# Cross-attention with a routed feed-forward layer: the stacks of key and query terms are laid out with the product term innermost, and the query stack is filled by transfers

## The reference, cut to what matters

```python
# x: (32, 100, 128), ctx: (32, 1444, 128), 16 heads of 8 dimensions, mask: (32, 100)
q = (layernorm(x) @ W_q.T)  # -> (32, 16, 100, 8)
k = (ctx @ W_k.T)           # -> (32, 16, 1444, 8)
v = (ctx @ W_v.T)           # -> (32, 16, 1444, 8)
scores = einsum('bhqd,bhkd->bhqk', q, k) / sqrt(8)
p = exp(clip(scores, -50, 50)); attn = p / p.sum(-1)     # masked query rows give 0
x = x + (einsum('bhqk,bhkd->bhqd', attn, v) as (32, 100, 128)) @ W_o.T
z = layernorm(x)            # then 8 experts (128 -> 512 -> 128, gelu), the best 2 of each token
x = x + sum over the best 2 of weight * (gelu(z @ w1[e]) @ w2[e])
```

## Time and profile before

| what | us |
|---|---|
| median of 3 runs | 1222.01 (1219.8 to 1224.07) |
| the profiled execution, its own time | 1223.99 |
| its span, from the first to the last instruction | 1221.9 |
| PE busy | 1079.1 (88%) |
| PEld busy | 780.2 (64%) |
| DVE busy | 822.9 (67%) |
| ACT busy | 750.4 (61%) |
| POOL busy | 256.4 (21%) |
| ACT, exponentials (L885) x512 | 589.2 |
| PE, score matmuls (L675) x1536 | 431.5 |
| DVE, clipping (L1040) x512 | 388.1 |

### The profile page before, as it was taken

How to read it: one execution, slowest core, us unless ns; L and a number is a source line. 1 busy time by engine, 2 the same in 40 slices (tenths; PEclk the granted TensorE clock), 3 DMA queues, 4 the chain that set the end, 5 groups by cost and what they waited for, 6 DMA issues and landing times.

```text
span 1221.9 us, 31043 instructions
## 1 busy us (share of the span) xinstructions
PE 1079.1 (88%) x10734; PEld 780.2 (64%) x10735; DVE 822.9 (67%) x2083; ACT 750.4 (61%) x959; POOL 256.4 (21%) x325
## 2 busy tenths in 40 slices
PE   4699999999999999999999999999999999869990
PEld 3466666666666666666666666666666666569990
DVE  4666667777777777777777777777777777644443
ACT  2576666666677666666666666666666676534440
POOL 2701111111111111111111111111111111225554
PEclk8799999999999999999999999999999999979995
DMA  6655665556666555555555566666666666312225
GB/s 150 149 122 136 145 146 136 134 129 137 144 144 141 136 135 135 136 134 135 135 135 132 136 138 144 144 144 144 144 144 137 135 133 149 105 48 65 65 58 162
DMA packets 89010, 159.58 MB, mean 131 GB/s; under 512 B 13792, under 2 KB 66020, under 8 KB 88980
## 3 DMA queue, kind: packets, MB, share of 16 engines
q1 hardware_dynamic: 84084, 152.55, 54.4%
q0 software_dynamic: 4896, 6.63, 2.0%
HBM read 36.83 MB, written 22.08 MB: 48 GB/s over the span
## 4 chain that ended last, share of the span: by engine, by line
PE 44%; SPq 25%; DMA 18%; ACT 4%; DVE 4%; issue 4%; POOL 0%; ACTq 0%; POOLq 0%; DVEq 0%
SPq L405 23%; DMA k_stack<-k_lo 16%; PE scores L675 11%; PE o_sum L687 11%; PE scratch L604 6%; PE scratch L599 5%; ACT k_full L852 4%; PE scores L791 4%; PE scores L802 4%; DVE k_lo L945 1%; DMA x_all<-in_x_dram 1%; SPq L464 1%; DVE k_hi L943 1%; PE scratch L618 1%; PE scores L781 1%
## 5 line engine op out<-in xcount | busy, mean ns | idle before, releaser
L885 ACT ACTIVATE probs<-scores 128x1200 f32<-128x1200 f32 x512 | 589.2, 1179 | 140.7 <-PE scores L675 137.9
L675 PE MATMUL scores<-q_stack,k_stack 128*128 128x400 f32 x1536 | 431.5, 395 | 44.6 <-DMA k_stack<-k_lo 39.4
L1040 DVE TENSOR_SCALAR probs<-probs 128x1200 f32<-128x1200 f32 x512 | 388.1, 784 | 53.7 <-ACT probs L885 52.6
L675 PEld LDWEIGHTS scores<-q_stack,k_stack 128*128 128x128 f32 x1536 | 255.8, 190 | 174.9 <-issue 109.8
L687 PE MATMUL o_sum<-probs,v_both 128*17 128x200 f32 x6144 | 317.9, 337 | 11.6 <-DVE probs L1040 11.5
L687 PEld LDWEIGHTS o_sum<-probs,v_both 128*17 128x17 f32 x6144 | 152.2, 97 | 106.6 <-DVE probs L1040 25.3
L558 POOL DMA_INDIRECT expert_rows<-rows,row_atu x64 | 78.1, 1220 | 451.5 <-DMA expert_rows<-fill 384.0
L618 PE MATMUL scratch<-w_turned,ctxT 128*128 128x128 f32 x768 | 108.8, 285 | 10.9 <-DVE v_both L976 7.3
L618 PEld LDWEIGHTS scratch<-w_turned,ctxT 128*128 128x128 f32 x768 | 95.9, 192 | 32.2 <-DVE v_both L976 17.7
L852 ACT COPY k_full<-scratch 128x512 f32<-128x512 f32 (+1 forms) x93 | 52.2, 561 | 93.7 <-PE scratch L604 93.7
L548 POOL TENSOR_SCALAR rstd<-moments 100x1 f32<-100x1 f32 x32 | 39.0, 1218 | 299.5 <-DVE moments L1078 299.5
(11 more groups left out here) (145 smaller groups left out, 861.9 us busy)
## 6 DMA issues: line engine op xcount, KB each, us to landing
k_stack<-k_hi SPq DMA_DIRECT2D x256, 192.0 KB, 4.7
k_stack<-k_lo SPq DMA_DIRECT2D x256, 192.0 KB, 5.5
expert_rows<-fill SPq DMA_DIRECT2D x32, 406.2 KB
xT_and_ctx<-in_ctx_dram SPq DMA_DIRECT2D x16, 704.0 KB
ctx_nat<-in_ctx_dram SPq DMA_DIRECT2D x16, 704.0 KB
v_both<-expert_rows SPq DMA_DIRECT2D x57, 65.0 KB, 1.8
xT_and_ctx<-in_L_ffn_w_dram SPq DMA_DIRECT2D x1, 2048.0 KB
w_sb<-in_L_ffn_w_dram SPq DMA_DIRECT2D x8, 256.0 KB
```

Source lines behind the costliest of these rows:

```text
L675: last = nc.tensor.matmul(scores[:, c % 2, m, 0:GQ], k_stack[p][:, g, t * P:(t + 1) * P], q_stack[p][:, g, :, :].rearrange("p h q -> p (h ...
L885: nc.scalar.activation(probs[:, c % RING, :, :], scores[:, c % 2, :, 0:GQ], ACT.Exp, scale=SCALE).then_inc(exp_ready, 1)
L1040: nc.vector.tensor_scalar(chunk, chunk, LOW, HIGH, ALU.max, ALU.min).then_inc(probs_ready, 1)
```

## The change

Three things change. (1) Inside both stacks the term is now the innermost index of the partition: partition 4*r + t instead of 32*t + r. So a transfer of `stack_keys` writes every fourth partition from t to 127. The key projection's columns are permuted once at the start (ACT's copy of `w_turned`), so that the 32 rows of group g are every fourth partition of `k_hi` and `k_lo` as well, and the transfer reads every fourth partition from g. Number and size of these transfers stay. (2) The query stack is no longer written by DVE: POOL clears both copies once at the start, and SP fills the four blocks that are not zero with four transfers (`stack_queries`), 32 partitions of 1600 bytes each, for every batch, behind the 16 of the keys. PE now waits for them as well (`QD`). DVE's low part is made on all 128 partitions with one instruction: q - hi where a column `minus_low` is -1, and q where it is 0. (3) `q_stack` has the head before the group, so that a matmul reads its 400 columns as 4 runs of 100 columns, 400 columns apart.

```diff
@@ -161,11 +162,11 @@
-        wq_rep = sb("wq_rep", [P, GROUPS, 4, HG * DH])
+        wq_rep = sb("wq_rep", [P, GROUPS, HG * DH, 4])
         q_parts = sb("q_parts", [P, GROUPS, SQ], F32R)
-        own_head = sb("own_head", [P, 4, HG])
-        head_mask = sb("head_mask", [P, HG])
-        q_stack = [sb(f"q_stack{p}", [P, GROUPS, HG, SQ], F32R) for p in range(2)]
+        own_low = sb("own_low", [P, HG * DH])
+        minus_low = sb("minus_low", [P, 1])
+        q_stack = [sb(f"q_stack{p}", [P, HG, GROUPS, SQ], F32R) for p in range(2)]
...
@@ -399,15 +401,24 @@
             def stack_keys(p):
 
-                R = HG * DH
                 for t, part in enumerate((k_hi, k_lo, k_hi, k_lo)):
                     for g in range(GROUPS):
-                        sp.dma_start(k_stack[p][t * R:(t + 1) * R, g, :].bitcast(F32),
-                                     part[g * R:(g + 1) * R, :].bitcast(F32)).then_inc(k_stacked, 16)
+                        sp.dma_start(k_stack[p][t:P:4, g, :].bitcast(F32),
+                                     part[g:P:GROUPS, :].bitcast(F32)).then_inc(k_stacked, 16)
+
+            def stack_queries(p):
+
+                R = 4 * DH
+                for h in range(HG):
+                    sp.dma_start(q_stack[p][h * R:(h + 1) * R, h, :, :].bitcast(F32),
+                                 q_parts[h * R:(h + 1) * R, :, :].bitcast(F32)).then_inc(q_stacked, 16)
 
             sp.wait_ge(cleared, 3)
             sp.wait_ge(k_split, KSTEPS)
             stack_keys(0)
+            sp.wait_ge(q_stack_cleared, 2)
+            sp.wait_ge(q_split, 1)
+            stack_queries(0)
...
@@ -423,6 +434,8 @@
                 sp.wait_ge(k_split, KSTEPS * (b + 2))
                 stack_keys(1 - p)
+                sp.wait_ge(q_split, b + 2)
+                stack_queries(1 - p)
...
@@ -488,15 +501,15 @@
-            nc.gpsimd.memset(own_head[:], 1.0).then_inc(own_head_step, 1)
...
+            nc.gpsimd.memset(own_low[:], -1.0).then_inc(own_low_step, 1)
...
+            for p in range(2):
+                nc.gpsimd.memset(q_stack[p][:].bitcast(F32), 0.0).then_inc(q_stack_cleared, 1)
...
@@ -608,7 +621,7 @@
-                                            wq_rep[:, g, :, :].rearrange("p t r -> p (t r)"),
+                                            wq_rep[:, g, :, :].rearrange("p r t -> p (r t)"),
...
@@ -674,7 +687,7 @@
                                             k_stack[p][:, g, t * P:(t + 1) * P],
-                                            q_stack[p][:, g, :, :].rearrange("p h q -> p (h q)"),
+                                            q_stack[p][:, :, g, :],
...
@@ -731,7 +744,7 @@
-                        pe.wait_ge(q_stacked, b + 2)
+                        pe.wait_ge(q_stacked, QD * (b + 2))
...
@@ -826,7 +839,10 @@
-            nc.scalar.copy(w_turned[:].rearrange("p n d -> p (n d)"), scores[:, 1, 2, :]
+            nc.scalar.copy(w_turned[:, WK, :].rearrange("p (h d g) -> p h d g", h=HG, d=DH),
+                           scores[:, 1, 2, WK * P:(WK + 1) * P].rearrange("p (g h d) -> p h d g", g=GROUPS, h=HG))
+            nc.scalar.copy(w_turned[:, WQ, :], scores[:, 1, 2, WQ * P:(WQ + 1) * P])
+            nc.scalar.copy(w_turned[:, WV:, :].rearrange("p n d -> p (n d)"), scores[:, 1, 2, WV * P:]
                            ).then_inc(w_turned_ready, 1)
...
@@ -945,31 +961,23 @@
-            def split_queries(p, b, step):
+            def split_queries(b, step):
 
                 dve.wait_ge(scratch_emptied, step + 1)
                 if later(b):
-                    dve.wait_ge(q_stacked, b)
+                    dve.wait_ge(q_stacked, QD * b)
                 flat = q_parts[:].rearrange("p g q -> p (g q)")
                 nc.vector.tensor_copy(flat, q_full[:]).then_inc(q_hi_ready, 1)
                 dve.wait_ge(q_hi_ready, b + 1)
-                nc.vector.tensor_tensor(flat[P // 2:P, :], q_full[P // 2:P, :],
-                                        flat[P // 2:P, :].bitcast(F32), ALU.subtract
-                                        ).then_inc(q_split, 1)
-                dve.wait_ge(q_split, b + 1)
-                if later(b, 2):
-                    dve.wait_ge(scores_ready, CHUNKS * (b - 1))
-                for h in range(HG):
-                    ins = nc.vector.tensor_scalar(q_stack[p][:, :, h, :], q_parts[:].bitcast(F32), head_mask[:, h:h + 1],
-                                                  None, ALU.mult)
-                ins.then_inc(q_stacked, 1)
+                nc.vector.scalar_tensor_tensor(out=flat, in0=flat.bitcast(F32), scalar=minus_low[:], in1=q_full[:],
+                                               op0=ALU.mult, op1=ALU.add).then_inc(q_split, 1)
```

More of the change, by code:

```diff
@@ L78, in xattn_moe @@
     KD = 16 * 4 * GROUPS
+    QD = 16 * HG
     QB = 4
@@ L283, in xattn_moe @@
         wq_rep_ready = sem("wq_rep_ready")
-        own_head_step = sem("own_head_step")
-        head_mask_ready = sem("head_mask_ready")
+        own_low_step = sem("own_low_step")
+        minus_low_ready = sem("minus_low_ready")
+        q_stack_cleared = sem("q_stack_cleared")
         q_hi_ready = sem("q_hi_ready")
@@ L489, in _ @@
                                     base=0, pattern=[[-1, P]], channel_multiplier=1).then_inc(ident_ready, 1)
-            nc.gpsimd.memset(own_head[:], 1.0).then_inc(own_head_step, 1)
[L492 to L499, removed]
+            nc.gpsimd.memset(own_low[:], -1.0).then_inc(own_low_step, 1)
+            pool.wait_ge(own_low_step, 1)
+            nc.gpsimd.affine_select(out=own_low[:], in_=own_low[:], compare_op=ALU.is_ge, fill=0.0, base=-2,
+                                    pattern=[[-4, HG * DH]], channel_multiplier=1).then_inc(own_low_step, 1)
+            pool.wait_ge(own_low_step, 2)
+            nc.gpsimd.affine_select(out=own_low[:], in_=own_low[:], compare_op=ALU.is_ge, fill=0.0, base=3,
+                                    pattern=[[4, HG * DH]], channel_multiplier=-1).then_inc(own_low_step, 1)
+            for p in range(2):
+                nc.gpsimd.memset(q_stack[p][:].bitcast(F32), 0.0).then_inc(q_stack_cleared, 1)
             pool.wait_ge(half_ready, 1)
@@ L721, in _ @@
             pe.wait_ge(mask_ready, 1)
-            pe.wait_ge(q_stacked, 1)
+            pe.wait_ge(q_stacked, QD)
             pe.wait_ge(k_stacked, KD)
@@ L836, in _ @@
             nc.scalar.copy(wq_rep[:], w_turned[:, WQ, :].rearrange("p (g r) -> p g r", g=GROUPS)
-                           .unsqueeze(2).broadcast_to([P, GROUPS, 4, HG * DH])).then_inc(wq_rep_ready, 1)
+                           .unsqueeze(3).broadcast_to([P, GROUPS, HG * DH, 4])).then_inc(wq_rep_ready, 1)
             def take(name, k, b, f, step):
@@ L955, in split_queries, with split @@
                 dve.wait_ge(q_hi_ready, b + 1)
-                nc.vector.tensor_tensor(flat[P // 2:P, :], q_full[P // 2:P, :],
-                                        flat[P // 2:P, :].bitcast(F32), ALU.subtract
-                                        ).then_inc(q_split, 1)
-                dve.wait_ge(q_split, b + 1)
-                if later(b, 2):
-                    dve.wait_ge(scores_ready, CHUNKS * (b - 1))
-                for h in range(HG):
-                    ins = nc.vector.tensor_scalar(q_stack[p][:, :, h, :], q_parts[:].bitcast(F32), head_mask[:, h:h + 1],
-                                                  None, ALU.mult)
-                ins.then_inc(q_stacked, 1)
-            def split(name, k, p, b, step):
+                nc.vector.scalar_tensor_tensor(out=flat, in0=flat.bitcast(F32), scalar=minus_low[:], in1=q_full[:],
+                                               op0=ALU.mult, op1=ALU.add).then_inc(q_split, 1)
+            def split(name, k, b, step):
                 if name == "key":
@@ L971, in split @@
                 if name == "query":
-                    split_queries(p, b, step)
+                    split_queries(b, step)
             def take_values(p, k, step):
@@ L1010, in _ @@
             nc.vector.tensor_copy(mask_rows[:], mask_u8[:]).then_inc(mask_cast, 1)
-            dve.wait_ge(own_head_step, 3)
-            nc.vector.tensor_reduce(head_mask[:], own_head[:].rearrange("p t h -> p h t"), AX.X, ALU.add
-                                    ).then_inc(head_mask_ready, 1)
+            dve.wait_ge(own_low_step, 3)
+            nc.vector.tensor_reduce(minus_low[:], own_low[:].unsqueeze(1), AX.X, ALU.add
+                                    ).then_inc(minus_low_ready, 1)
+            dve.wait_ge(minus_low_ready, 1)
             moments_of(0)
@@ L1022, in _ @@
                 if r == 3:
-                    split_queries(0, 0, ALONE.index(("query", 0)))
+                    split_queries(0, ALONE.index(("query", 0)))
             for r in range(2, DVE_NORMS):
@@ L1158, in attend @@
                     if c:
-                        split(*planned(b, c - 1), 1 - p, b + 1, scratch_step(b, c - 1))
+                        split(*planned(b, c - 1), b + 1, scratch_step(b, c - 1))
```

## The result

The changed kernel takes 1166.92 us (median of 4, 1166.3 to 1167.3) against 1222.06 us (median of 4): a ratio of 0.9549 with a 95% interval of 0.9532 to 0.9566.

A forecast was written before the change was run, and what follows sets the result against it. Two loops were taken to share a batch's period: PE's work and the keys' way through DVE, SP and DMA. Stack waits 29.0, clip waits 11.5 and start 2.5 gave 43 us off 1224.0; forecast 1180 us, range 1170 to 1228.

The forecast's parts named there:

- What bounds the kernel, and why the transfers are slow: PE and the keys' way share the period; 32 neighbouring partitions reach 8 of 16 ports, giving 207 GB/s against 377.
- The rate of the stepped transfers: Key and query transfers into the stacks: rate taken from the upper end, 377 GB/s, with bounds of 200 and 377.
- this rival: Engines still meet at the ports in stepped transfers, so the rate lies between; 1202 us at 230 GB/s; chance 0.14.
- The other rival: Stepped key transfers stay at about 207 GB/s, four more precede PE's wait; 1254 us, 1271 at 200; chance 0.14.
- SP: SP's 20 issues at 0.63 to 0.69 us, 2.3 for the last landing: stacks complete after 14.3 to 15.4 us.
- DVE: Four multiplications (1.44 us) go, the new subtraction takes 0.57; PE's 0.38 us wait for a clip goes.
- PE's four runs, POOL's and ACT's edits: Matmul reads in 4 runs of 100 columns, POOL's clears and ACT's weight copies at the start: all taken as free.
- The start: PE's first scores come at 38.5 to 39.6 us instead of 41.96; gain 2.4 to 3.5, taken as 2.5.
- The sum: Whole kernel: 29.0 + 11.5 + 2.5 = 43 us off the profiled 1224.0, so 1181; 1180 is the forecast.
- its two terms for the waits, 29.0 and 11.5: PE's waits ahead of scores: 29.0 us for the key stack in 28 later batches, 11.5 for 30 waits for clips.
- the step brings no rate: Stepped key transfers stay slow: stacks complete at 18.0 us, 1.0 later, 31 times and at the start; 1254 us; chance 0.14.
- That DVE's gain is worth nothing while the transfers hold the loop: Relieving DVE of the query-stack multiplications gains nothing if the key transfers keep their slow rate.

The follow-up runs named there:

- neighbours: The changed kernel with key transfers moving 32 neighbouring partitions on both sides again (output not the reference's); 1314.7 us, ratio 1.0738 to the kernel before.
- keys_only: The changed kernel with the query stack written by four DVE multiplications as before, without query transfers; 1183.94 us, ratio 0.9690 to the kernel before.
- dve_back: The changed kernel plus four unused DVE multiplications of 400 columns behind the query split, batches 2 to 30; 1183.25 us, ratio 0.9684 to the kernel before.
- no_mults: The kernel before without DVE's four query-stack multiplications from batch 2 on (output not the reference's); 1233.12 us, ratio 1.0108 to the kernel before.
- q_halves: The changed kernel with each of the four query transfers cut into two halves, same bytes; 1217.66 us, ratio 0.9947 to the kernel before.
- eight: The changed kernel with its 16 key transfers merged into 8, each to 64 partitions in steps of two; 1163.01 us.

## Why the prediction was right and where it failed

- **What bounds the kernel, and why the transfers are slow:** right. The engines, not SP's issue, held the rate, and the partitions set it (neighbours against the change, 210 against 407 GB/s at full share).
- **The rate of the stepped transfers:** right; 377 was taken, 407 found. With the step on both sides nothing is left of the low rate, so this rival is out; with it on one side only, the rate stays below (264 and 134), for a reason that no run shows. The other rival left open whether 32 partitions with a step are as good as a span of all of them; on both sides, they are here.
- **SP:** right. 0.64 us an issue; four query transfers land 1.9 us after issue (2.3 taken).
- **DVE:** 0.64 us for the new instruction instead of 0.57; the clip's wait is gone all the same.
- **PE's four runs, POOL's and ACT's edits:** nothing, as taken. The start gave 3.3 us (2.5 taken).
- **The sum: here it failed, in its two terms for the waits, 29.0 and 11.5, and in one that it did not have.** First, the waits were sized by the idle column, which counts from the modelled end of a matmul. From start to start they were 1.04 and 0.57 us in a late batch, not 0.97 and 0.38; that is some 6 us for 25 late batches. keys_only and dve_back measured the larger size for DVE's part, 0.6. Second, the 29.0 counted 28 waits for the stacks where there were 31: three, 4.8 us, stood in another row of the table. Third, a term was missing: a wait of PE can also cost the clock behind it. Three stretches at half clock, 1.6 us each, went with the waits, another 5 us. The profile before showed them: a granted clock of 0.95 over each of three early batches, and periods of 34 us. The start gave 1 us more than its term; 1 us of waits stayed in the early batches, and the tail took nearly 3 back. 43 + 6 + 5 + 5 + 1 - 1 - 3 = 56, against the measured 56.7. So every wait that was to go did go, and the direction was right for the reason given; what failed is the size put on the waits and the clock that was put at nothing.
- **The rival "the step brings no rate":** its mechanism stands as described (neighbours complete the stacks after 18.1 us, 18.0 written), but its price of 32 us was 92. Most of the difference is the missing term: this run has 30 stretches at half clock behind its waits, 7 of them of double length, so 34 more than the kernel before; at 1.6 us each they are 54 of the missing 60 us.
- **That DVE's gain is worth nothing while the transfers hold the loop:** right in the period (no_mults: 31.85), and with the clock even a loss.

## What to carry to other kernels

For transfers inside SBUF of 32 rows of 6 KB, try to spread the rows over all partitions on both sides: here a step of four on source and destination doubled the rate, a step of two within one half did nothing, and a step on one side alone gave little or made it worse. It costs only a permutation of rows, which a projection's weights can carry. Price a wait of PE by the distance between the starts of the matmuls around it, compared with a place where nothing is waited for, look at the granted clock behind it, and check that the number of waits in the table is the number of times that the loop waits. Two waits on one loop don't add: the one that is hidden (DVE's here) became worth 17 us only when the other was gone.

## What the hardware showed that was not expected

- Destination stepped, source of 32 neighbours: 264 GB/s at full share; source stepped, destination of neighbours: 134; both neighbours: 210; both stepped: 407. The asymmetry is not explained.
- In all these runs, every stretch at half clock between the first batch and the tail began at the end of a wait of PE for the stacks or just behind it, and each one of 3.4 us cost 1.6 us. The shortest such wait was 1.56 us. The 26 late waits of about 1.0 us before the change had no stretch behind them, nor had those of 1.2 us in q_halves. With longer waits it varies: of 26 late waits of 1.5 to 1.6 us in no_mults three had one, the last wait before the change (2.1 us) had none, and of the 31 waits in neighbours, most of them of 2.6 us, 30 had one.
- A read of every source row twice in one transfer (eight) moves 384 KB to 64 partitions and lands after 3.9 us in the median.
